# Telling the loader that a weight slot is free: by a small product of its own, or by the next block's first product

## The reference, cut to what matters

```python
# layer 1 (_L1_ffn_ref): a dense MLP for 506 patch tokens, and small two-way experts for 6 class tokens
patch_out = gelu(patch_tokens @ fc1_w.T + fc1_b) @ fc2_w.T + fc2_b
hid_all = gelu(einsum('bnd,ahd->bnah', cls_tokens, atom_in_w) + atom_in_b)
route_candidates = einsum('bnrh,nrdh->bnrd', sh_pair, route_out_w) + atom_out_b[dst]
# layer 3 (_L3_ffn_ref): eight experts, 64 tokens each, one expert per token
h = gelu(einsum('ecd,edm->ecm', expert_inputs, w1) + b1[:, None, :])
expert_outputs = gelu(einsum('ecm,emd->ecd', h, w2) + b2[:, None, :])
out = einsum('ecd,tec->td', expert_outputs, combine)
```

## Time and profile before

| | us |
|---|---|
| median of three runs | 3429.54 |
| the three runs | 3431.44, 3426.95, 3429.54 |
| the profiled execution, its own time | 3425.07 |
| its span, from the first instruction to the last | 3422.9 |
| the stretch of `ffn1` on TensorE | 1936.9 to 2016 |
| the stretch of `ffn3`'s blocks on TensorE | 3318.3 to 3387.9 |

### The profile page before, as it was taken

The page is one execution under the profiler, slowest core; times in us unless marked ns, Lnnn a source line. Parts: engine busy times, 40 slices in busy tenths (PEclk is TensorE's granted clock), DMA queues, the critical chain, the costliest instruction groups (busy, mean ns, idle before and its releaser), DMA issues.

```text
span 3422.9 us, 39533 instructions
## 1 busy us (share of the span) xinstructions
PE 3111.7 (91%) x14175; PEld 2448.5 (72%) x14175; DVE 1743.7 (51%) x2919; ACT 749.5 (22%) x1315; POOL 1425.4 (42%) x1007
## 2 busy tenths in 40 slices
PE   8999798999999968989766789989999998989978
PEld 3576577888888855768645558768888886778857
DVE  7735698465555354347575455543333446741131
ACT  1044111233332222112133212121111112221222
POOL 2021288344434433645500025436666664436500
PEclk9999898999999989999978779999999999999986
DMA  2011365112212211222200132213323332113313
GB/s 79 19 47 38 111 208 188 51 56 75 65 56 63 76 56 44 85 68 74 83 0 9 42 97 74 74 58 95 98 87 101 96 92 74 59 51 101 92 48 111
DMA packets 91267, 256.99 MB, mean 75 GB/s; under 512 B 10335, under 2 KB 10975, under 8 KB 90852
## 3 DMA queue, kind: packets, MB, share of 16 engines
q1 hardware_dynamic: 80352, 219.45, 21.2%
q10 hardware_dynamic: 10788, 35.83, 3.0%
HBM read 253.67 MB, written 1.57 MB: 75 GB/s over the span
## 4 chain that ended last, share of the span: by engine, by line
PE 83%; DVE 10%; issue 3%; ACT 2%; POOL 1%; DMA 0%; DVEq 0%; ACTq 0%; POOLq 0%
PE ps L415 22%; PE ps L419 21%; PE ps L420 21%; PE ps L893 2%; PE ps L519 1%; DVE aux L1823 1%; PE ps L513 1%; PE ps L1000 1%; PE ps L1128 1%; PE ps L1031 1%; PE ps L772 1%; PE ps L783 1%; PE ps L765 1%; PE ps L757 1%; DVE hot L2172 1%
## 5 line engine op out<-in xcount | busy, mean ns | idle before, releaser
L363 POOL TENSOR_SCALAR w_hi<-raw 128x768 fp32r<-128x768 f32 x498 | 457.7, 919 | 1774.9 <-PE ps L415 1452.3
L366 POOL TENSOR_TENSOR w_lo<-raw,w_hi 128x768 fp32r<-128x768 f32 x498 | 976.0, 1960 | 41.5
L415 PE MATMUL ps<-H_hi,w_hi 128*128 128x512 f32 x804 | 318.8, 396 | 20.5 <-issue 15.5
L419 PE MATMUL ps<-H_lo,w_hi 128*128 128x512 f32 x804 | 316.7, 394 | 0.0
L420 PE MATMUL ps<-H_hi,w_lo 128*128 128x512 f32 x804 | 316.5, 394 | 0.0
L415 PE MATMUL ps<-B_hi,w_hi 128*128 128x512 f32 x720 | 291.8, 405 | 21.1 <-DVE B_lo L1619 14.9
L415 PE MATMUL ps<-A_hi,w_hi 128*128 128x512 f32 x780 | 307.8, 395 | 1.8 <-DVE sel_now L2094 1.8
L419 PE MATMUL ps<-A_lo,w_hi 128*128 128x512 f32 x780 | 304.7, 391 | 0.0
L420 PE MATMUL ps<-A_hi,w_lo 128*128 128x512 f32 x780 | 304.2, 390 | 0.0
L419 PE MATMUL ps<-B_lo,w_hi 128*128 128x512 f32 x720 | 283.3, 393 | 0.0
L420 PE MATMUL ps<-B_hi,w_lo 128*128 128x512 f32 x720 | 282.7, 393 | 0.0
(11 more groups left out here) (439 smaller groups left out, 5926.1 us busy)
## 6 DMA issues: line engine op xcount, KB each, us to landing
raw<-stream_dram SPq DMA_DIRECT2D x558, 384.0 KB, 3.1
w_ring<-w_dram ACTq DMA_DIRECT2D x39, 384.0 KB, 3.6
u_rows<-rows_dram ACTq DMA_DIRECT2D x8, 768.0 KB, 6.2
rows<-rows_dram ACTq DMA_DIRECT2D x7, 768.0 KB, 4.0
w_last<-w_dram ACTq DMA_DIRECT2D x9, 384.0 KB, 3.7
x<-x_dram ACTq DMA_DIRECT2D x1, 1536.0 KB, 9.7
out_dram<-x ACTq DMA_DIRECT2D x1, 1536.0 KB, 5.1
orf<-orf_dram ACTq DMA_DIRECT2D x6, 192.0 KB, 3.0
```

Of the source, the lines that this page charges most:

```text
L363: pool.tensor_scalar(w_hi[:, b // 3, b % 3], raw[:, b // 3, b % 3], 1.0, 1.0, ALU.mult, ALU.mult)\
L366: pool.tensor_tensor(w_lo[:, b // 3, b % 3], raw[:, b // 3, b % 3], w_hi[:, b // 3, b % 3], ALU.subtract)\
L415: mm = pe.matmul(o, wh, xh, start=first, stop=False, skip_group_check=True)
L419: pe.matmul(o, wh, xl, start=False, stop=False, skip_group_check=True)
```

## The change

The small product is left out for all but the last block of each of the two parts. `whole_block_used` now only counts a block as owed. The first product of the next block (`k == 0`) adds the owed number to `raw_used` when it ends, through `raw_given_back`. TensorE ends its products in order, so the finished first product says that the block before it is done as well. Padding blocks have no products, so q=15, 16 and 17 of `ffn3` are given back together, three at once, by the first product of the output layer. The block ahead of `degrees()` is given back by the first product behind it. The calls with `last` keep the small product, since no block follows them.

```diff
-            def whole_block_used():
-                pe.matmul(ps[0:2, 7, 0:2], ones_b[:, :], ones_b[:, :], start=True, stop=True,
-                          skip_group_check=True).then_inc(raw_used, 1)
+            raw_owed = [0]
+
+            def whole_block_used(last=False):
+                raw_owed[0] += 1
+                if last:
+                    raw_given_back(pe.matmul(ps[0:2, 7, 0:2], ones_b[:, :], ones_b[:, :], start=True, stop=True,
+                                             skip_group_check=True))
+
+            def raw_given_back(mm):
+
+                if raw_owed[0]:
+                    mm.then_inc(raw_used, raw_owed[0])
+                    raw_owed[0] = 0
...
                             mm = pe.matmul(ps[:, f, c], raw[:, f // 3, f % 3, k], acc[:, k, c], start=k == 0,
                                            stop=k == KC - 1, skip_group_check=True)
+                            if k == 0:
+                                raw_given_back(mm)
                         done(mm, f, "act")
                         whole_block_used()
...
-                        whole_block_used()
+                            if n == 1 and k == 0:
+                                raw_given_back(mm)
+                        whole_block_used(n == 1 and f == KC - 1)
                         if (n, f) == (1, 0):
                             degrees()
...
                         done(mm, f, "act")
-                        whole_block_used()
+                        whole_block_used(n == 2 and f == KC - 1)
```

## The result

The changed kernel takes 3410.16 us, the median of five runs (3409.44 to 3415.08); the kernel before took 3429.3 in its five. The ratio is 0.9954, with a 95% interval of 0.9943 to 0.9964: 0.46% faster (the ratio is estimated from all fast runs of both kernels, and is not the quotient of the two medians). The prediction was 3425.1 within 3417 to 3431, so it missed, on the fast side. The profiled execution took 3410.36 us, its span 3408.2.

What follows compares the result with a forecast made beforehand. TensorE was taken as the bound: busy 91% of the span, 83% of the chain. Removing 50 small products gains 4.71 us, less 0.3 lost behind degrees: 4.4 net, from the median 3429.54 to 3425.1, range 3417 to 3431.

Steps and rivals of the forecast that it cites:

- The sum's first term: Layers 1 and 3: removing 50 small products on the path, about 0.094 us each, gains 4.71 us.
- my upper bound, the bar of 0.164: One small product costs at most its whole bar, 0.164 us; 8.2 us for all 50.
- a wait that is met costs nothing: Layer 3's first block, a wait ahead of each product, takes 1.34 us, the next 1.48; so waits add 0.
- a block's own pieces have the same length with and without waits: Chain pieces of blocks: the reason given for pricing a small product at the chain's 0.094 us.
- Back-to-back issue gap: Skill's estimate for products up to 64 columns: 25 ns each, 1.3 us for the 50; the trace's 0.09 was preferred.
- Where the removed products were on the path: 18 in layer 1 (1.68 us) and 32 in layer 3 (3.03 us) count; three between layer 3's groups gain nothing.
- the five behind degrees: Layer 1: removing these small products gains nothing, as they lie under VectorE's work to 2020.98.
- Slots given back later: Rows of blocks: release moves some 0.1 us in a 7.4 us cycle, covered by over 3 us.
- The load wait at the fourth output block: Layer 3's output group: later release of slot 3 may cost 0 to 1 us; taken as 0.
- Behind degrees: Layer 1: GpSimd's earlier splits shift against VectorE's work, between 0.5 us gained and 1.8 lost; 0.3 lost taken.
- a clock that stays up: Layer 3's output group: denser blocks keep the granted clock from falling, 16.9 us more gained, 3408; chance 0.10.
- The slower rival: Layer 3's hidden group: the clock falls there, 19 us lost less the 4.4 gained, 3444; chance 0.05.

Runs made afterwards that it cites:

- two_small: The kernel before with two small bf16 products behind each unsplit block, the first adding to no semaphore: 3428.15 us, ratio 1.0005.
- mute_small: The changed kernel with the small bf16 product put back between blocks, adding to no semaphore: 3426.34 us, ratio 0.9998.
- fill_late: The changed kernel with four extra f32 products in the pause between layer 3's groups, waits left in place: 3395.71 us, ratio 0.9907.
- fp32r_split: The changed kernel with the small product that reports split blocks used in fp32r, 2 stationary columns, instead of bf16: 3406.76 us, ratio 0.9938.
- wide_bf16_split: The changed kernel with the small product that reports split blocks used in bf16 with 128 stationary columns: 3406.66 us, one run.

## Why the prediction was wrong

- The sum's first term was mis-sized. It was 50 small products of 0.094 us, 4.71 in all; they measured about 11.9 us: 0.235 and 0.287 in layer 3 at the full and the half clock, 0.19 to 0.29 in layer 1. The chain's piece behind L408 is only the small product's own step. The pieces on either side held the rest: 93 ns of waiting in the last pass of the block ahead and 48 ns in the first of the block behind. Even my upper bound, the bar of 0.164, was too low.
- The sum had no term for the clock, which I held to be unchanged outside the rivals. It gave 4.4 us: 1.1 in layer 1's hidden group, 1.8 at degrees, 1.5 in the last stretch. Without it, by estimate, the time would still have been some 7 us below the forecast (11.9 gained for 4.7).
- The step that failed was the reading of the earlier trace rows: "a wait that is met costs nothing", from 1.34 us for the first block and 1.48 for the next. The first block differs in a second way: no small product stands ahead of it or inside the start of its piece. The difference of 0.14 us was what I was looking for, 0.093 + 0.048, and I read it as the absence of a cost. The sentence on waits itself is right (with a wait ahead of each product, the block's twelve passes start within 1.233 us, where eleven steps of 0.112 are 1.23); it doesn't say what the small product costs. Likewise "a block's own pieces have the same length with and without waits" compared blocks that all had a small product beside them.
- The rule of the Trainium skill that I weighed (TensorE: Matmul & The Clock Gate, "Back-to-back issue gap": 25 ns for a product of few columns) was right about the product and not about its place: two_small puts a second one at 26 ns. I had set it against the 0.09 and gone by the trace, where both were parts of 0.235.
- Where the removed products were on the path was right: 18 in layer 1, 32 in layer 3, nothing for the three between the groups, where only the waits changed. For the five behind degrees, VectorE's stretch doesn't show any loss or gain beyond 0.4 us.
- Slots given back later: right. mute_small has the late release and the time of before. The load wait at the fourth output block, 0 to 1 us, doesn't show at the half clock. In fill_late, at the full one, TensorE stands still for 0.16 us there, and from start to start the step is 0.32 longer.
- Behind degrees I took 0.3 us lost within 0.5 gained to 1.8 lost; VectorE's stretch became 0.4 shorter.
- The new waits' price I had not counted: 0.3 us between the groups, with the two waits that moved to the first output product.
- The rival "a clock that stays up" named 3408, close to what came, by a road that wasn't taken: the clock fell after two to three output blocks as before. That the number came out near is luck. Less time at the half clock came in three places that I hadn't named: layer 1's hidden group, degrees and the tail, 4.4 us. The mechanism itself is real, as the filled pause shows, and it named the pause. The slower rival, a clock that falls in layer 3's hidden group, didn't happen in any profile.

## What to carry to other kernels

A tiny product put between large ones is priced by the distance from the last regular start before it to the second regular start behind it, less the regular steps, not by its own bar or its piece of the chain. A product that only signals can be replaced by an addition on the next product; where it must stay, bf16 with 128 stationary columns or fp32r cost 0.055 us here where two columns in bf16 cost 0.235. And where the clock falls behind a pause between two groups of narrow products, fill the pause: here four idle products of 64 columns were worth 14 us. A wait that is moved to an earlier instruction can stop the engine there, as the two moved waits did.

## What the runs showed of the hardware that I had not expected

- The weight load of a single 2-column bf16 stationary operand, and the first of an f32 one, started within 2 ns of its product, and so did the load of the f32 block behind it. The other loads in these rows started 0.025 us or more ahead of their product: 0.056 inside a block, 0.11 for bf16 with 128 columns.
- In rows of 512 moving columns the product behind a small one takes 0.31 to 0.34 us to its successor where 0.227 is usual: 0.34 behind bf16 with 2 columns, 0.31 behind the other three forms. I have no experiment on that rest of 0.09.
- One and the same small product cost 0.19, 0.235 or 0.29 us at the full clock, by the moving columns (8, 64 or 512) of the products beside it.
- The same 192 output products of 64 columns ran to their end at the full clock behind a filled pause (six profiles) and once behind one of 0.74 us. Behind 1.01 us, behind 0.40 + 0.74, and behind 0.48 to 0.64 in kernels with small products, the clock fell 2 to 3 us into the group, or in fp32r_split and wide_bf16_split at its first product. What decides is open; the runs give only these points.
